# A convolution's output step divided anew between ScalarE, GpSimd and VectorE

## The reference, cut to what matters

```python
x = x + window_attention(group_norm(x))    # 7x7 windows, shifted by 3, 8 heads
x = x + conv3x3(group_norm(x), w)          # 3x3, 'SAME', 128 -> 128 channels
```

## Time and profile before

| | |
|---|---|
| median of 3 runs | 3809.45 us (3807.93 to 3814.52) |
| the profiled execution, from its first to its last instruction | 3811.0 us |
| busy: PE, DVE, ACT, POOL | 92%, 81%, 69%, 61% of the span |
| mean granted clock of TensorE | 0.972 of full speed |

### The profile page before, as it was taken

The page is one execution under the profiler, slowest core; times in us unless marked ns, Lnnn a source line. Parts: engine busy times, 40 slices in busy tenths (PEclk is TensorE's granted clock), DMA queues, the critical chain, the costliest instruction groups (busy, mean ns, idle before and its releaser), DMA issues.

```text
span 3811.0 us, 154831 instructions
## 1 busy us (share of the span) xinstructions
PE 3499.2 (92%) x57227; PEld 2843.6 (75%) x57227; DVE 3074.2 (81%) x7552; ACT 2642.8 (69%) x5857; POOL 2316.9 (61%) x3674
## 2 busy tenths in 40 slices
PE   2999999999999999999999999999999999999997
PEld 1677777777777777777777777777777777777775
DVE  5788877888878888788888788887788887888885
ACT  1877776777766677767777667767767777677773
POOL 4476555666555665556765556655556655566663
PEclk9999999999999999999999999999999999999998
DMA  2011110111101111101111101111011111111001
GB/s 54 19 32 34 32 30 24 31 32 34 32 25 27 34 34 32 32 22 32 32 34 34 27 25 32 34 33 33 22 29 32 34 34 27 27 30 34 17 17 30
DMA packets 213494, 115.45 MB, mean 30 GB/s; under 512 B 8784, under 2 KB 212688, under 8 KB 212688
## 3 DMA queue, kind: packets, MB, share of 16 engines
q1 hardware_dynamic: 212688, 104.72, 10.5%
HBM read 53.31 MB, written 51.38 MB: 27 GB/s over the span
## 4 chain that ended last, share of the span: by engine, by line
POOL 48%; issue 38%; PE 7%; DVE 3%; POOLq 2%; ACT 1%; SPq 0%; DMA 0%; DVEq 0%; ACTq 0%
POOL s_sb L408 21%; POOL plane L436 11%; POOL x_n L448 7%; POOL x_n L425 4%; PE conv_ps L998 2%; PE qkv_ps L879 2%; POOL gn_t L392 1%; POOL gn_t L394 1%; PE attn_ps L917 1%; POOL gn_t L393 1%; POOL gn_y L395 1%; PE probsT_ps L903 1%; PE scores_ps L892 1%; POOLq L388 1%; POOLq L405 1%
## 5 line engine op out<-in xcount | busy, mean ns | idle before, releaser
L408 POOL TENSOR_TENSOR s_sb<-s_sb,s_max 113x392 f32<-113x392 f32 x1024 | 1028.1, 1004 | 1304.8 <-DVE s_max L752 1304.4
L464 ACT ACTIVATE probs<-s_sb 113x392 f32<-113x392 f32 x1024 | 551.7, 539 | 195.6 <-POOL s_sb L408 136.9
L903 PE MATMUL probsT_ps<-ident,probs 113*128 113x113 f32 x4096 | 596.6, 269 | 77.8 <-ACT probsT L470 77.7
L470 ACT COPY probsT<-probsT_ps 128x392 f32<-128x392 f32 x1024 | 490.1, 479 | 189.2 <-PE probsT_ps L903 181.5
L917 PEld LDWEIGHTS attn_ps<-v,probsT 128*49 128x49 f32 x16384 | 472.3, 127 | 199.2 <-issue 142.5
L436 POOL TENSOR_TENSOR plane<-x_n 128x224 f32<-128x224 f32 x896 | 591.9, 681 | 30.3 <-POOL x_n L425 23.3
L752 DVE TENSOR_REDUCE s_max<-s_sb 113x8 f32<-113x392 f32 x1024 | 574.8, 561 | 35.4
L531 ACT COPY v<-qkv_ps 64x256 f32<-64x256 f32 (+2 forms) x1280 | 394.1, 328 | 287.2 <-PE qkv_ps L879 281.0
L917 PE MATMUL attn_ps<-v,probsT 128*49 128x34 f32 x16384 | 575.0, 215 | 14.1 <-DVE o_sb L723 11.6
L747 DVE TENSOR_TENSOR s_sb<-scores_ps,bias 113x392 f32<-113x392 f32 x1024 | 566.2, 553 | 13.2 <-PE scores_ps L892 12.5
L892 PE MATMUL scores_ps<-k,q 32*49 32x98 f32 x16384 | 473.6, 254 | 79.8 <-issue 79.8
(11 more groups left out here) (142 smaller groups left out, 6776.6 us busy)
## 6 DMA issues: line engine op xcount, KB each, us to landing
x_in<-in_x_dram SPq DMA_DIRECT2D x224, 224.0 KB, 2.9
out_dram<-x_out SPq DMA_DIRECT2D x224, 224.0 KB, 2.5
x_b<-in_L_conv_w_dram SPq DMA_DIRECT2D x1, 576.0 KB
x_b<-L_conv_pruning_mask_dram SPq DMA_DIRECT2D x1, 576.0 KB
x_n<-_conv_rel_pos_table_dram SPq DMA_DIRECT2D x14, 10.7 KB
x_n<-in_mask_dram SPq DMA_DIRECT2D x1, 196.0 KB
w_in<-n_L_conv_qkv_weight_dram SPq DMA_DIRECT2D x1, 192.0 KB
ident<-in_ident_dram SPq DMA_DIRECT2D x1, 64.0 KB
```

Of the source, the lines that this page charges most:

```text
L408: nc.gpsimd.tensor_tensor(s, s, top, ALU.subtract).then_inc(sub_ready, 1)
L464: nc.scalar.activation(probs[0:QP, slot % 2, :, :, 0:N], s_sb[0:QP, slot % 4], ACT.Exp)\
L470: nc.scalar.copy(probsT[:, slot % 2], probsT_ps[:].rearrange("p (w n) -> p w n", n=ODD)[:, :, 0:N])\
L903: last = nc.tensor.transpose(probsT_ps[:, w * 128:w * 128 + QP], probs[0:QP, u % 2, w].rearrange("p e m -> p (e m)"), ident[0:QP, 0:QP])
```

## The change

The weights are laid out anew so that planes 0 and 1 are the two middle ones of the Winograd form (the sum and difference planes), 2 and 3 the outer ones, and the last plane's weights are negated. PE now multiplies planes 0, 1, 2, 3 in this order. In the third unit of a tile ACT scales both middle planes out of PSUM in one instruction (`m_mid`, 448 elements a partition where L508 had 224). In the same unit, after its planes, POOL forms their sum and difference (`both`, two instructions of 224 elements). In the fourth unit DVE adds x (`with_x`, 448 elements, both inputs in SBUF), waits for that, and forms `result = plane * scale + with_x` over both outer planes (448 elements, one input in PSUM). PE's first matmul of a tile now waits for ACT's `m_mid` of the tile before, its nineteenth for the last tile's `result`. `result` is kept as two stacks of rows, so the turned tile has another order of rows, and SP issues four DMAs of a quarter of the size each.

```diff
-PLANE_ORDER = (1, 0, 2, 3)
...
-        out_tiles = out.rearrange("n (t a) w c -> n t (a w) c", t=TILES).rearrange("n t (s p) c -> n t p s c", p=SP_)
+        out_tiles = out.rearrange("n (t h r a) w c -> n t a r w h c", t=TILES, h=2, r=2, a=2)
...
# SP
-                            sp.dma_start(out_tiles[img, t], x_out[:, t * SUB:(t + 1) * SUB, :]).then_inc(x_stored[t], 16)
+                            for a in range(2):
+                                for r in range(2):
+                                    sp.dma_start(out_tiles[img, t, a, r], x_out[r * W:(r + 1) * W, t * SUB + 2 * a:t * SUB + 2 * a + 2, :])\
+                                        .then_inc(x_stored[t], 16)
...
# POOL, behind its planes
-                        sums = ((d[0], d[2], ALU.subtract), (d[1], d[2], ALU.add),
-                                (d[2], d[1], ALU.subtract), (d[1], d[3], ALU.subtract))
+                        sums = ((d[1], d[2], ALU.add), (d[2], d[1], ALU.subtract),
+                                (d[0], d[2], ALU.subtract), (d[1], d[3], ALU.subtract))
...
+                    for t in range(TILES):
+                        turn, at = half_done(t)
+                        if u == at and live(i, -1 - turn):
+
+                            number = (i - 1 - turn) * TILES + t
+                            pool.wait_ge(mid_ready, number + 1)
+                            need(pool, with_x_ready, number)
+                            for a, op in enumerate((ALU.add, ALU.subtract)):
+                                nc.gpsimd.tensor_tensor(both[:, a], m_mid[:, 0], m_mid[:, 1], op).then_inc(both_ready, 1)
...
# ACT
-                            need(act, conv_sums, number * 4)
-                            nc.scalar.copy(m_1[:], conv_ps[:, 1, 0:PP]).then_inc(m1_ready, 1)
+                            need(act, both_ready, number * 2)
+                            nc.scalar.activation(m_mid[:], conv_ps[:, 0:2, 0:PP], ACT.Identity, scale=wc_scale[:])\
+                                .then_inc(mid_ready, 1)
...
# DVE, third unit of a tile
-                            dve.wait_ge(m1_ready, number + 1)
-                            need(dve, conv_sums, number * 4)
-                            vec.tensor_tensor(m_sum[:], m_1[:], conv_ps[:, 0, 0:PP], ALU.add).then_inc(conv_sums, 1)
...
# DVE, fourth unit of a tile
+                            dve.wait_ge(both_ready, (number + 1) * 2)
+                            dve.wait_ge(xc_ready, (img + 1) * len(XC_AT))
+                            need(dve, conv_out, number)
+                            vec.tensor_tensor(with_x[:].rearrange("p a (r w) -> p a r w", w=W),
+                                              both[:].rearrange("p a (r w) -> p a r w", w=W),
+                                              flat(x_c)[:, t * TP:(t + 1) * TP]
+                                              .rearrange("p (r a w) -> p a r w", a=2, w=W), ALU.add).then_inc(with_x_ready, 1)
+                            dve.wait_ge(with_x_ready, number + 1)
                             dve.wait_ge(conv_ready, number + 1)
-                            vec.tensor_tensor(m_diff[:], m_1[:], m[2], ALU.subtract).then_inc(conv_sums, 1)
-                            vec.tensor_tensor(y[0], m[2].rearrange("p (r w) -> p r w", w=W),
-                                              m_sum[:].rearrange("p (r w) -> p r w", w=W), ALU.add).then_inc(conv_sums, 1)
-                            vec.tensor_tensor(y[1], m_diff[:].rearrange("p (r w) -> p r w", w=W),
-                                              m[3].rearrange("p (r w) -> p r w", w=W), ALU.subtract).then_inc(conv_sums, 1)
...
-                            vec.scalar_tensor_tensor(out=result[:], in0=conv_y[:].rearrange("p r a w -> p (r a w)"),
-                                                     scalar=wc_scale[:], in1=flat(x_c)[:, t * TP:(t + 1) * TP],
+                            vec.scalar_tensor_tensor(out=result[:].rearrange("p a r w -> p a (r w)"),
+                                                     in0=conv_ps[:, 2:4, 0:PP], scalar=wc_scale[:], in1=with_x[:],
                                                      op0=ALU.mult, op1=ALU.add).then_inc(conv_out, 1)
...
# PE
                     if n == 0:
-                        need(pe, conv_sums, (img * TILES + k) * 4)
+                        need(pe, mid_ready, img * TILES + k)
+                    if n == 2 * 3 * KW:
+                        need(pe, conv_out, img * TILES + k)
```

More of the change, by code:

```diff
@@ L198, in build_block @@
         x_c = sb("x_c", [128, H, W])
-        result = sb("result", [128, TP])
+        result = sb("result", [128, 2, TPAIRS, W])
         x_n = sb("x_n", [128, H + 2, W])
@@ L205, in build_block @@
         plane_lo = sb("plane_lo", [128, PLANES, H // 2, PAD], F16)
-        m_1, m_sum, m_diff = sb("m_1", [128, PP]), sb("m_sum", [128, PP]), sb("m_diff", [128, PP])
-        conv_y = sb("conv_y", [128, TPAIRS, 2, W])
+        m_mid = sb("m_mid", [128, 2, PP])
+        both = sb("both", [128, 2, PP])
+        with_x = sb("with_x", [128, 2, PP])
         x_out = sb("x_out", [SP_, TILES * SUB, C])
@@ L280, in build_block @@
         conv_ready = sem("conv_ready")
-        m1_ready = sem("m1_ready")
-        conv_sums = sem("conv_sums")
+        mid_ready = sem("mid_ready")
+        both_ready = sem("both_ready")
+        with_x_ready = sem("with_x_ready")
         conv_out = sem("conv_out")
         x_tiles = x.rearrange("n (t a) w c -> n t (a w) c", t=TILES).rearrange("n t (s p) c -> n t p s c", p=SP_)
-        out_tiles = out.rearrange("n (t a) w c -> n t (a w) c", t=TILES).rearrange("n t (s p) c -> n t p s c", p=SP_)
+        out_tiles = out.rearrange("n (t h r a) w c -> n t a r w h c", t=TILES, h=2, r=2, a=2)
         def flat(t):
@@ L491, in misc @@
                         act.wait_ge(misc_ready, number + 1)
-                        need(act, x_stored[t], 16 * img)
+                        need(act, x_stored[t], 4 * 16 * img)
                         nc.scalar.copy(x_out[:, t * SUB:(t + 1) * SUB, :],
@@ L645, in _ @@
             u0, u1, u2, u3 = (wc_u[:, KW * j:KW * (j + 1), :] for j in range(PLANES))
-            step(vec.tensor_tensor(u0, g0, g2, ALU.add))
-            step(vec.tensor_tensor(u1, u0, g1, ALU.add))
-            step(vec.tensor_tensor(u2, u0, g1, ALU.subtract))
-            step(vec.tensor_scalar(wc_u[:, KW:3 * KW, :], wc_u[:, KW:3 * KW, :], 0.5, None, ALU.mult))
-            step(vec.tensor_copy(u0, g0))
-            step(vec.tensor_copy(u3, g2))
+            step(vec.tensor_tensor(u2, g0, g2, ALU.add))
+            step(vec.tensor_tensor(u0, u2, g1, ALU.add))
+            step(vec.tensor_tensor(u1, u2, g1, ALU.subtract))
+            step(vec.tensor_scalar(wc_u[:, 0:2 * KW, :], wc_u[:, 0:2 * KW, :], 0.5, None, ALU.mult))
+            step(vec.tensor_copy(u2, g0))
+            step(vec.tensor_scalar(u3, g2, -1.0, None, ALU.mult))
             step(vec.tensor_copy(wc_hi[:], wc_u))
@@ L765, in body @@
                         vec.tensor_copy(flat(x_c)[:, t0 * TP:t1 * TP], flat(x_b)[:, t0 * TP:t1 * TP]).then_inc(xc_ready, 1)
-                    for t in range(TILES):
-                        turn, at = half_done(t)
-                        if u == at and live(i, -1 - turn):
-                            number = (i - 1 - turn) * TILES + t
-                            dve.wait_ge(m1_ready, number + 1)
-                            need(dve, conv_sums, number * 4)
-                            vec.tensor_tensor(m_sum[:], m_1[:], conv_ps[:, 0, 0:PP], ALU.add).then_inc(conv_sums, 1)
                     for kind, t in misc_at(i, u - 1):
@@ L960, in misc @@
                     for s in range(SUB):
-                        last = nc.tensor.transpose(misc_ps[0:SP_, s * C:(s + 1) * C], result[:, s * SP_:(s + 1) * SP_], ident[:])
+                        last = nc.tensor.transpose(misc_ps[0:SP_, s * C:(s + 1) * C], result[:].rearrange("p a r w -> p (a r w)")[:, s * SP_:(s + 1) * SP_], ident[:])
                 if kind == "ot":
@@ L987, in conv @@
                 for n in range(first, first + CONV_PARTS[at][place]):
[L989 removed]
+                    j, (part, dx) = n // (3 * KW), divmod(n % (3 * KW), KW)
                     if n == 0:
[L991 removed]
+                        need(pe, mid_ready, img * TILES + k)
+                    if n == 2 * 3 * KW:
+                        need(pe, conv_out, img * TILES + k)
                     half, rest = divmod(n, 2 * 3 * KW)
```

10 lines of the change are left out of this document (1 added, 9 removed).

## The result

The changed kernel took 3821.46 us (median of eight runs, 3819.80 to 3822.22), the kernel before 3812.18 us beside it: a ratio of 1.0027, with an interval of 1.0017 to 1.0037. It is slower by 9.3 us, where 20.6 were forecast; 3821 lies inside the range of 3800 to 3860. The profiled execution took 3821.94 us, with a span of 3820.1.

The account below looks back on a forecast made before the run. The prediction took PE, 92% busy, to set the pace. Loop 12.6 plus end 8.0 gave 20.6 us on the profiled 3811.0, so 3831.6, median 3830; the 8-in-10 range was 3800 to 3860.

Parts of the forecast that it names:

- the loop's term: Three places in each image together cost +0.42 us; over 30 images +12.6 us.
- The end: Last image's convolution, with no attention beside it, gets longer behind POOL's queue: +8 us, from +5 to +11.
- The third tile: In the last image, its last DVE instruction starts at about 3790.2 us instead of 3784.28, +5.9 us.
- The last four tiles: In the last image, a new chain over ACT, POOL and DVE adds +0.25 us a tile, +1.0 in all.
- PE's longer idling: In the last image PE idles longer; what that costs behind it was put at 0.6 us, between 0 and 2.
- Place one: Units 6 to 8: one held gn_var, +0.26 us, against unit 7's shorter output step, -0.26: net 0.0 an image.
- The third rival: Each two-input DVE instruction waits for a whole POOL instruction: +0.85 us at unit 6's gn_var, 3864 us; chance 0.16.
- Place two: Units 22 and 23: POOL's both delays the subtraction and Newton steps, +0.15 us an image, between -0.3 and +0.5.
- Place three: Units 26 and 27: ACT's longer copy delays L470, so PE waits +0.27 us an image, between 0.18 and 0.33.
- Worth nothing there: DVE's saving over 224 tiles, some 125 us, falls nearly all beside a busy PE and gains nothing.
- The first rival: Faster: POOL's additions fit idle time, nothing is held, both long waits shrink: -0.86 us an image, 3792 us; chance 0.20.
- The likeliest case: The forecast itself, slower: places at 0.0 to +0.8 us an image, end at 5 to 11; 3818 to 3842; chance 0.42.

Follow-up runs that it names:

- the one-input form: The changed kernel with gn_dev and both gn_var written with one tensor input, other operands one value per partition: 3777.87 us, 0.9912 of before.
- the fills: The changed kernel with two 320-column memsets of a scratch tile added on DVE for each tile: 3833.17 us, 1.0052 of before.
- the sums of u = 6 first: The changed kernel with POOL's two sums of unit 6 issued ahead of that unit's subtraction instead of behind it: 3815.67 us, 1.0014 of before.
- ACT's shorter instruction: The changed kernel with ACT taking out only one middle plane (224 columns), which POOL uses twice: 3815.32 us, 1.0009 of before.
- the one-input form in the kernel before: The kernel before with gn_dev and both gn_var written with one tensor input: 3809.12 us, 0.9995 of before.
- the last image's sums on DVE: The changed kernel with the two sums of the last image's seven tiles formed by DVE instead of POOL: 3816.00 us, 1.0014 of before.
- the delay: The kernel before with six more gn_var-like instructions into a scratch tile ahead of the second norm's two: 3827.17 us, 1.0037 of before.

## Why the prediction was right in sign and wrong in size, point by point

The forecast was 20.6 us slower; measured were 9.3. The step that failed is the loop's term, "Together +0.42 us an image; 30 images have all three, +12.6 us": it took the passage from one image to the next as it was. From unit 6 to unit 30 an image lost 0.29 us, the passage gave 0.29 back, and the loop came out at 0. The sign came true by the end alone.

**The end: right.** Forecast +8.0, measured +9.1. Of this 1.76 arose in the attention of the last image, behind which no loop boundary follows, and belongs to the images by the forecast's own division; the end's own part is 7.4. The third tile: +5.9 forecast, 7.25 less the 1.76, so 5.5. The last four tiles: +1.0 forecast, as 0.25 each; three of them took 5.33 us instead of 5.41, 0.08 less each. For what PE's longer idling costs I had 0.6, between 0 and 2: the first of the four tiles took 7.17 us instead of 5.41, because PE came back from 4.43 us of waiting at a granted clock of 0.50 (3791.2 to 3798.0; 1.07 us for the four transposes instead of 0.62). For the DMA issues I had 0.5: 0.34 more behind the last DVE instruction.

**The loop: forecast +12.6, measured 0.** At a like clock its size was nearly right, 0.32 us an image for 0.42, or 10 us. That is luck, for it is made of other terms.

Place one failed as a cause. It was the sum of +0.26 for one held `gn_var` and -0.26 for the shorter output step, so 0.0. I took the unheld first `gn_var` of unit 21 against the rule of the Trainium skill, page "SBUF — State Buffer", section "Who interferes with whom". Measured were +0.85 at unit 7 for the pair, in which each `gn_var` ended with a half of `both`, and -0.33 at unit 8: +0.52. The trace agrees with the rule there, and with its other half, that a VectorE instruction with at most one SBUF input, outside the two-port performance modes, does not contend: in the one-input form 0.46 us instead of 1.20. Why the first `gn_var` of unit 21 passed stays open; POOL's instruction there has one tensor input, `both` has two. The third rival named this mechanism, but that its +0.85 is the measured figure is chance: it had taken the 0.26 off already, and by its own mechanism the pair takes 1.28 us instead of 0.35, so the hold would be 0.93 and not 1.1.

Place two: +0.15 forecast, +0.21 measured. Place three: +0.27 forecast, +0.26 in PE's transposes. The prediction looked for it as a third row of waits, and none came: PE's matmuls in front of these transposes run until 2462.97, and an idle time of 0.11 us is too short for the list.

"Worth nothing there", of DVE's 125 us, was the second cause that failed. The unit-7 step apart, which the forecast counts in place one, the lighter queue gave 0.24 in unit 20, and the fills took some 0.9 us an image back. And of the 125 us, holds left 24. The 0.65 at unit 28, of which 0.25 is left by unit 30, is not the queue's length, since the fills did not touch it; it was not tried further.

**The clock** was in no term. It was low at 13 boundaries instead of 24, so that the passage fell from 31.78 to 31.49 us on the mean, which is the loop's whole loss. The runs with two images in a pass, where the distance between the kernels is 19.3 us, come near the 20.6 of the forecast for this reason; that says that its terms add up, not that each was right.

The first rival, faster, named the right point, the `gn_var` of unit 6. With the hold taken away the change gives 31 us, where that rival had 18 (3809 to 3792); its price of -0.86 us an image was about right: at a like clock an image took 115.24 us with the one-input form, against 116.14 before.

The likeliest case's range of 3818 to 3842 is that of the places alone, with the end at 8.0; with the end at 5 to 11 it is 3814 to 3844. And the 1.55 us taken off at the end of the sum is the distance of a span from a time: in the changed kernel the profiled run took 3821.94 us at a span of 3820.1, so a span lies some 2 us below its own run's time.

## What to carry to other kernels

Work moved to GpSimd is not free because GpSimd idles: look at which small two-input instruction of VectorE falls beside it, and whether someone waits for that. Here it could be written with one tensor input, and the change became a gain. And where a loop has idle passages at which the clock falls, a few microseconds of difference between two kernels say little about their work: compare the stretch between two such passages, or images at a like clock, or take passages away.

## What the hardware showed that was not expected

Copies of 392 columns from SBUF to SBUF on DVE, with one input, took 0.83 us on the mean at one of the two places, where fills of 320 took 0.325 and copies beside which POOL had nothing running 0.35: they too were held by POOL. The Trainium skill, page "SBUF — State Buffer", section "Who interferes with whom", lists copies among the instructions that can take the shared port pair, which agrees.

The two sums cost POOL 1.27 us and DVE 0.69 where it works alone, but DVE 1.62 beside POOL's planes.

At the loop boundaries the granted clock repeats in a pattern: low at nearly all in the kernel before, at every second one in the changed kernel, at 27, 18 and 5 of 27 in three of the experiments. PE's idle time does not tell them apart: 2.81 to 3.43 us ahead of the low ones, 2.80 to 3.41 ahead of the others. A delay of 0.8 us was enough to turn most of them. Most surprising is how well the passage fills up what units 6 to 30 leave: these take 83.70 us on the mean with the sums of u = 6 first, 83.76 with ACT's shorter instruction, 83.95 with the one-input form in the kernel before, 84.26 in that kernel, 84.54 in the changed one and 84.60 with the last image's sums on DVE, and yet an image with its passage is 116.01 to 116.07 us long in all six. Outside this band, with 83.03 (one-input form) and 85.25 (the delay), it is 114.77 and 116.45. What sets this stays open.
